# Graph network, one core: edge tables split while the linear makes them, target parts per block, and a sum of 49 products placed by TensorE alone

## What is computed

```python
x = _layernorm(x + _L0_gnn_ref(x, edge_index, ...))                 # hypergraph convolutions
x = _layernorm(x + _L1_gnn_ref(x, edge_attr_64, ..., src, dst))
x = _layernorm(x + _L2_gnn_ref(x, edge_index, ...))
x = _layernorm(x + _L3_gnn_ref(x, edge_index))                      # normalised sum over neighbours

# L1, per edge, D = 64, H = 128:
edge_in = concatenate([edges, nodes[receivers], nodes[senders]])
h = relu(edge_in @ We1 + be1);  new_edges = h @ We2 + be2
agg = segment_sum(new_edges, receivers)
new_nodes = relu(concatenate([agg, nodes]) @ Wn1 + bn1) @ Wn2 + bn2
# L2, per edge:
k, q, v = x @ W_key + b_key, x @ W_query + b_query, x @ W_value + b_value
msg = sigmoid(k[dst] + q[src]) * v[src]
out = segment_sum(msg, dst) + x @ W_skip + b_skip
```

## Time and profile before

| | us |
|---|---|
| median of 3 runs | 5276.46 (5270.39 to 5276.75) |
| profiled execution | 5276.83, its span 5274.8 |
| mean granted TensorE clock | 0.933 |
| PE busy / DVE / ACT / POOL | 4474.7 / 3575.7 / 2488.1 / 2635.9 |

### The profile page before, as it was taken

One profiled execution on the slowest core, in us unless ns is written; L12 is line 12 of the kernel. 1 busy time (PEld: TensorE's weight loads), 2 busy tenths in 40 slices (PEclk: granted clock), 3 DMA queues, 4 the chain that ended last, 5 costly groups with the idle time before them and its releaser, 6 DMA issues.

```text
span 5274.8 us, 160095 instructions
## 1 busy us (share of the span) xinstructions
PE 4474.7 (85%) x61948; PEld 4075.5 (77%) x61948; DVE 3575.7 (68%) x5668; ACT 2488.1 (47%) x3821; POOL 2635.9 (50%) x2387
## 2 busy tenths in 40 slices
PE   1777799969999849999999999999758888888587
PEld 1666788869999848888888888888557777777577
DVE  6999888841110247767676767767459999999812
ACT  0333799940000146656565656666235555555400
POOL 0488655556666766666667666661003333333200
PEclk9677899989999979999999999999769999999888
DMA  5996688899999665555555555554045444554396
GB/s 122 222 223 142 219 320 320 321 284 406 377 418 417 256 208 171 163 173 164 172 171 166 171 158 176 169 165 145 26 136 159 154 152 152 152 150 150 106 365 269
DMA packets 802884, 1105.90 MB, mean 210 GB/s; under 512 B 428155, under 2 KB 708081, under 8 KB 794988
## 3 DMA queue, kind: packets, MB, share of 16 engines
q1 hardware_dynamic: 721658, 986.29, 56.9%
q0 software_dynamic: 73696, 111.71, 6.7%
q10 hardware_dynamic: 7056, 0.91, 0.1%
HBM read 788.30 MB, written 314.35 MB: 209 GB/s over the span
## 4 chain that ended last, share of the span: by engine, by line
PE 53%; issue 18%; DVE 11%; DMA 7%; POOL 6%; ACT 4%; SPq 1%; DVEq 0%; POOLq 0%; ACTq 0%
PE PS L1060 10%; PE PS L1169 8%; PE PS L1145 8%; PE PS L1149 8%; PE PS L1156 7%; POOL arena L696 6%; PE PS L1097 3%; PE PS L1128 3%; PE PS L996 2%; DMA arena<-cnt_t 2%; DVE arena L1748 2%; ACT arena L1351 1%; PE PS L835 1%; ACT arena L1355 1%; PE PS L1005 1%
## 5 line engine op out<-in xcount | busy, mean ns | idle before, releaser
L762 POOL DMA_INDIRECT feat_slot<-SK,sidx_p x1764 | 2124.6, 1204 | 1120.0 <-DMA feat_slot<-SK,sidx_p 613.1
L1145 PE MATMUL PS<-arena 128*128 128x128 bf16 x14406 | 1448.3, 221 | 82.7 <-DVE arena L1987 57.5
L1149 PE MATMUL PS<-arena 128*128 (+2 forms) x14406 | 1407.4, 207 | 2.5 <-issue 2.5
L1145 PEld LDWEIGHTS PS<-arena 128*128 128x128 bf16 x14406 | 983.7, 99 | 97.0 <-issue 78.9
L1149 PEld LDWEIGHTS PS<-arena 128*128 128x128 bf16 x14406 | 951.2, 99 | 3.4 <-issue 3.2
L696 POOL TENSOR_TENSOR arena<-arena 128x448 bf16<-128x448 f32 x343 | 359.4, 1048 | 1024.7 <-ACT arena L1463 1024.7
L2007 DVE TENSOR_TENSOR arena<-arena 128x896 f32<-128x896 f32 (+1 forms) x686 | 586.2, 855 | 390.8 <-ACT arena L1454 385.2
L1169 PE MATMUL PS<-arena 128*128 128x384 bf16 (+1 forms) x4802 | 708.0, 288 | 146.8 <-POOL arena L696 143.6
L1463 ACT ACTIVATE arena<-arena 128x896 bf16<-128x896 f32 (+1 forms) x686 | 523.7, 763 | 561.5 <-DVE arena L2007 559.2
L1060 PE MATMUL PS<-arena 128*128 128x192 bf16 (+1 forms) x7203 | 613.9, 248 | 106.7 <-DVE arena L1845 62.3
L1060 PEld LDWEIGHTS PS<-arena 128*128 128x128 bf16 x7203 | 605.8, 98 | 113.5 <-DVE arena L1845 62.7
(11 more groups left out here) (238 smaller groups left out, 5778.8 us busy)
## 6 DMA issues: line engine op xcount, KB each, us to landing
arena<-slot_rows SPq DMA_DIRECT2D x1372, 224.0 KB
arena<-cnt_t SPq DMA_DIRECT2D x147, 896.0 KB
arena<-cnt_t SPq DMA_DIRECT2D x147, 672.0 KB
feat_slot<-zero SPq DMA_DIRECT2D x7, 10976.0 KB, 115.8
cnt_t<-arena SPq DMA_DIRECT2D x49, 1568.0 KB
cnt_s<-arena SPq DMA_DIRECT2D x49, 1568.0 KB
arena<-feat_slot SPq DMA_DIRECT2D x343, 224.0 KB
SK<-in_edge_attr_dram POOLq DMA_DIRECT2D x196, 288.0 KB
```

The costliest lines, as they stand in the source:

```text
L762: pool.indirect_dma_start(feat_slot, bass.IndirectOffsetOnAxis(ap=sidx_p[odd][:, n:n + 1].bitcast(u32), axis=0), fwin[h][:, t * D:(t + 1) ...
L1145: last = nc.tensor.matmul(PS[:, to:to + P], selS[c][:, cut], qsplit[:, (b * 3 + s) * H:(b * 3 + s + 1) * H], start=s == 0 and (k != 4 or j ...
L1149: last = nc.tensor.matmul(PS[:, to:to + w_], selT[c][:, cut], dsplit[:, bass.ds(w * (3 * w_) + s * w_, w_)], start=False, stop=k != 4 and ...
```

## The change

1. **Placing.** The two additions are gone; TensorE adds all 49 pieces with the identity, 49 matmuls where there were 13.
2. **Source parts unit by unit.** `tables(name)` replaces the linear's copies: per unit ScalarE copies to `NV` and to the first part, VectorE subtracts in `NV`, ScalarE makes the second part, VectorE the third, straight into `qsplit`. The source table no longer goes through DRAM (only in the general case, which these inputs don't take).
3. **Target table in pieces.** SP stores `NW` in four pieces as units are kept, and loads `dtab` in seven; block 0's slot rows and features are loaded ahead, at the linear's start (`first_slots`).
4. **Target parts per block in the pass.** `dsplit` shrinks to two buffers of one block. For block w + 1, ScalarE does `own_first` behind chunk 3 and `own_second` behind chunk 5 of block w, VectorE `own_residual` at the end of chunk 4 and `own_third` at the end of chunk 6; TensorE's first `meet` of a block waits for it (`dparts_dve`).
5. Buffers move in the arena, and `blocks` writes its last two blocks out.

```diff
@@ place_edges, TensorE and VectorE
-                    for n, b in enumerate(list(range(12)) + [NB - 1]):
+                    for b in range(NB):
                         last = nc.tensor.matmul(PS[:, 2560:2560 + WT], identb[:, :], prod[:, b * WT:(b + 1) * WT],
-                                                start=n == 0, stop=n == 12)
+                                                start=b == 0, stop=b == NB - 1)
...
-                    for n, ins in enumerate((
-                            lambda: TT(prod, before, ohx[odd], ALU.mult),
-                            lambda: TT(prod[:, 0:24 * WT], prod[:, 0:24 * WT], prod[:, 24 * WT:48 * WT], ALU.add))):
-                        ins().then_inc(slot_step, 1)
-                        dve.wait_ge(slot_step, w * 2 + (NB + n + 1))
-                    TT(prod[:, 0:12 * WT], prod[:, 0:12 * WT], prod[:, 12 * WT:24 * WT], ALU.add).then_inc(prod_made, 1)
+                    TT(prod, before, ohx[odd], ALU.mult).then_inc(prod_made, 1)
@@ SyncE
+            def store_table(k):
+                w, name = W_TAB[k], TABLES[k]
+                for lo, hi in ((0, 4), (4, 8), (8, 11), (11, UNITS[name])):
+                    at = slice(unit_blocks(name, lo)[0], unit_blocks(name, hi - 1)[-1] + 1)
+                    sp.wait_ge(lin_kept, units_before[name] + hi)
+                    sp.dma_start(tab[k].rearrange("(p b) f -> p b f", p=P)[:, at, :], NW[:, at, 0:w]).then_inc(tab_stored, 16)
...
-                sp.dma_start(dtab[:, 0:NB * w_].rearrange("p (b f) -> p b f", b=NB), tab[k].rearrange("(b p) f -> p b f", p=P))\
-                    .then_inc(tabs_in[0], 16)
-                sp.dma_start(qtab, nodes(tab_src[k])).then_inc(tabs_in[1], 16)
-                sp.wait_ge(splits_lo, 2 * NC * (m + 1))
...
+                for g in range(NC):
+                    sp.dma_start(dtab[:, g * CH * w_:(g + 1) * CH * w_].rearrange("p (b f) -> p b f", b=CH),
+                                 tab[k][g * CH * P:(g + 1) * CH * P, :].rearrange("(b p) f -> p b f", p=P))\
+                        .then_inc(tabs_in[int(g > 0)], 16)
...
+                with sp.If(fast):
+                    first_slots(k)
+                store_table(k)
+                with sp.If(fast):
+                    slots(k)
@@ slots, TensorE
-                pe.wait_ge(splits_lo, 2 * NC * (m + 1))
+                pe.wait_ge(splits_lo, UNITS["l1pq"] * (m + 1))
...
+                    if c == 0:
+                        pe.wait_ge(dparts_dve, w * 2 + (2 * NB * m + 2))
...
-                                                    dsplit[:, bass.ds(w * (3 * w_) + s * w_, w_)],
+                                                    dsplit[odd][:, s * w_:(s + 1) * w_],
@@ ScalarE, linear_split, per unit
+                        nc.scalar.activation(NV[:, bs_[0]:bs_[-1] + 1, :], o, ACT.Copy)
+                        nc.scalar.activation(q3[:, bs_[0]:bs_[-1] + 1, 0, :], o, ACT.Copy).then_inc(lin_kept_q, 1)
+                        if u > 0:
+                            second(u - 1)
@@ VectorE, units_split, per unit
+                        f(of(u), o).then_inc(lin_kept, 1)
+                    if 1 <= u <= UNITS[name]:
+                        dve.wait_ge(lin_kept_q, base + u)
+                        V.tensor_tensor(NV[:, of(u - 1), :], NV[:, of(u - 1), :], q3[:, of(u - 1), 0, :], ALU.subtract)\
+                            .then_inc(splits_res, 1)
+                    if u >= 2:
+                        dve.wait_ge(splits_mid, base + u - 1)
+                        V.tensor_tensor(q3[:, of(u - 2), 2, :], NV[:, of(u - 2), :], q3[:, of(u - 2), 1, :], ALU.subtract)\
+                            .then_inc(splits_lo, 1)
@@ slots, ScalarE's body
                         elif not first:
                             messages(w - 1, NC + c - 2, 1 - odd)
+                        if c == 3 and not (isinstance(w, int) and w == NB - 1):
+                            own_first(w + 1, 1 - odd)
+                        if c == 5 and not (isinstance(w, int) and w == NB - 1):
+                            own_second(w + 1, 1 - odd)
@@ slots, VectorE
+                def own_residual(w, odd):
+
+                    dve.wait_ge(dparts_act, w * 2 + (2 * NB * m + 1))
+                    own = dtab[:, bass.ds(w * w_, w_)]
+                    V.tensor_tensor(own, own, dsplit[odd][:, 0:w_], ALU.subtract).then_inc(dparts_dve, 1)
...
                             last_part(*old)
+                        if c == 4 and not (isinstance(w, int) and w == NB - 1):
+                            own_residual(w + 1, 1 - odd)
                         if c == 5 and not first:
                             second_part(w - 1)
+                        if c == 6 and not (isinstance(w, int) and w == NB - 1):
+                            own_third(w + 1, 1 - odd)
```

199 lines of the change are left out of this document (117 added, 82 removed).

## The result

The changed kernel took 5246.0 us (median of 17 runs, 5232.5 to 5269.1), the kernel before 5276.3 beside it: a ratio of 0.9944 [0.9932, 0.9956], 30 us. When it was measured again (e11) it was 0.9951 [0.9934, 0.9968]. Forecast were 69 us: the range's end, 5245, was missed by one. The profiled execution of the changed kernel took 5247.4 us (span 5245.8).

A forecast was written before the change was run, and what follows sets the result against it. VectorE was taken to bound placing and pass 5, TensorE pass 4. Terms -40 (placing), -59 and -48 (tables), 0 (pass 4's loop), +1 (features), +77 (pass 5's loop) gave -69: 5276.8 to 5208 us, range 5145 to 5245.

The forecast's parts named there:

- Features at the end of pass 4: Pass 4's end: features written by GpSimd would be just covered when block 48 needs them; +1 us (0 to +15).
- GpSimd goes at its own pace through all stages: Feature writes, placing to pass 4: GpSimd's pace was taken as its own, so its end would barely move.
- It ends where it did: Last feature writes: same end less about 8 us for an earlier start, so features are there at about 3583.
- The cover: Block 48: features 27 us late, against 20.6 us between issue and use, less 3, and some 8 TensorE is behind.
- Placing: Stage before counting: VectorE's two additions go, TensorE gets 36 more matmuls per block; -40 us (-46 to +43).
- The reserve for TensorE's half clock: Placing: at half clock throughout, TensorE needs 9.5 us per block; bound +43, rival time 5291 us, chance 0.03.
- Tables: Between linear and first product: -59 us before pass 4 (-50 to -63), -48 us before pass 5 (-42 to -50).
- the rival at 5228: Pass 4's linear not granted the clock it had: 5228 us; no chance of its own, inside the forecast's 0.72.
- Pass 4's loop: Two instructions more per block on ScalarE and VectorE, hidden behind TensorE: 0 us (0 to +10).
- Pass 5's loop: Two new VectorE instructions per block held behind GpSimd: +77 us (+5 to +99); rival for nothing 5136 us, chance 0.14.
- The change did what it says: Against a rival that store or loads still wait in the tables: -107 shrinks to about -60, 5255 us, chance 0.05.
- The clock in pass 5: Rival: longer TensorE waits bring half clock, 13 us per block; 5338 us at ten blocks, chance 0.06.

The follow-up runs named there:

- e11: The changed kernel, unaltered, measured again on the same chip as e9 and e10: 5257.2 us, 0.9951 of the kernel before.
- e2: Changed kernel with one wait more: VectorE waits for its own product in block 9 of placing. 5230.4 us, 0.9904 of the kernel before.
- e1: Changed kernel with placing undone (two VectorE additions, 13 identity matmuls back), the tables' part kept: 5278.0 us, 1.0003 of the kernel before.
- e4c: Changed kernel without the feature writes of the last three blocks and SyncE's wait for them: 5182.8 us, 0.9817 of the kernel before.
- e5c: Changed kernel with VectorE waiting for its own product in every block of placing: 5234.8 us, 0.9916 of the kernel before.
- e8c: Changed kernel with target parts' instructions moved to where GpSimd idles, in pass 5 alone, and e5c's waits: 5177.4 us, 0.9795 of the kernel before.
- e9: Changed kernel with e8c's moved instructions, first two blocks' row numbers made after three placing blocks, VectorE waits in blocks 3 to 9: 5157.1 us, 0.9756.
- e10: e9 with four indirect DMAs in flight in blocks 26 to 48, not three: 5113.8 us, 0.9686 of the kernel before.
- e3: Changed kernel with target parts' instructions moved to where GpSimd is idle, in passes 4 and 5: 5210.8 us, 0.9878 of the kernel before.
- e6c: Kernel before with the placing part alone, the tables as before: 5278.6 us, 1.0015 of the kernel before.

## Why the prediction was wrong

**Features at the end of pass 4: the step that failed**, +53 for +1, bound 15. Three errors add up in it. *"GpSimd goes at its own pace through all stages"*: it does not. A write took 1.7 us in layer 0 and 1.9 in pass 4 already before, and when placing was changed its writes slowed: by 518 us there were 120, where there had been 146. The held first write is 19 of the 26 (e2 got them back), slower writes behind it are the rest; with the additions (e1) all 26 are back. *It ends where it did*: even with those 19 back and 907 writes made by 1935 us, as many as before, e2's last one came at 3607, 18 us later than before, since each of the last 857 took 1.95 us and not 1.93; why is open. In the changed kernel it came 33 us later. *The cover*: I counted 8 us that TensorE is behind VectorE as slack. From the use of block 48's rows to the load of the sums it is 54.8 us before and 57.2 after, so there was none. My own 3583, a write, 3 us of load and those 54.8 make 3642, 11 us over the pass's own end at 3730 - 99 = 3631; that much was to be had from the rows of before. By the distance that seven profiles keep (last write plus 64.3 to 64.6 us) it is 17.

**Placing.** -52.7 for -40: TensorE kept up, the clock rose as expected (0.91). The reserve for TensorE's half clock wasn't needed, and a block became 1.06 us shorter (8.63 to 7.57), not 0.94, which times 49 is 52: from the product to the rank one-hots it was 2.04 us and is 0.99, and the sum had left out the small gap behind the product. What I took for the safe part was the one that made the writes late, and alone it gave nothing.

**Tables.** -49 for -48 in pass 5. In pass 4 -41 for -59: the stretch behind the linear lost 64 us, but the linear was granted half clock and took 23 us more, the rival at 5228. It is at full clock in e1, e2, e4c, e5c, e8c, e9 and e10, and at half in e3, e6c and e11.

**Pass 4's loop.** 0, right (e4c).

**Pass 5's loop.** Mechanism right, size 63 for 77: the 96 instructions cost 1.26 us each with their waits (121), the selects gave back 53 us in all, as counted (96 x 0.53 is 51), and the gates' own waits for ScalarE another 6. `own_residual` took 0.89 us and not the 1.0 of L2028, and 0.77 had been rounded to 0.8. The Trainium skill, page "SBUF — State Buffer", section "Who interferes with whom", has the rule for this: a two-input VectorE instruction stands for a GpSimd one that reads SBUF. The runs agree, bf16 operands included: 1.01 and 0.89 us behind GpSimd, 0.22 beside an idle one. The same section says that such instructions don't contend with one that only writes, and infers that descriptor generation is of that kind. The writes of placing speak against leaning on that here: beside nothing but such instructions the first took 47.1 us and the later ones 2.0 on average, where late in the changed kernel's pass 4, with VectorE standing, they took 0.97. That the port is the reason isn't shown.

**Rivals.** The change did what it says. The clock in pass 5 didn't fall (0.99). No rival had the feature writes as the next bound with a price of 50 us: the range ended at 5245 since I had given that cover 15 us at most. Of the signs of being wrong that the prediction names, one came: pass 4 ended with an idle TensorE, idle for 75 of the window's 1847 us where it had been for 37 of 1805.

## What to carry to other kernels

Before shortening stages ahead of a deadline, take the slowest background chain (here the last write plus 64.6 us) and ask how far it is from binding when everything ahead moves up; and don't assume that it keeps its pace when the stage beside it is changed. Small instructions that stand for another engine's are to be put where that engine is idle: the same work cost 9 us and not 63. Two parts that gain nothing alone may gain together, so a part's price isn't its own until the next bound is known.
